# Attention's norm of half 0 ahead of half 1's mixing, and gathered rows added around the wait for the turned gates

## The reference, cut to what matters

```python
x = x + 0.5 * ffn(layernorm(x))            # L0: r = sigmoid(xr W_r), out = r * (relu(xk W_k)^2 W_v)
x = x + attention(layernorm(x))            # L0: 8 heads of 16, bias, softmax over 1,024 keys
x = x + 0.5 * ffn(layernorm(x))            # L0 again
x = x + 0.5 * experts(layernorm(x))        # L1: router, best 2 of 16 experts
x = x + gated_delta_attention(layernorm(x))  # L1
x = x + 0.5 * experts(layernorm(x))        # L1 again
```

## Time and profile before

| what | us |
|---|---|
| median of 3 runs | 602.33 |
| lowest and highest | 601.64 and 602.38 |
| the profiled execution, its own time | 601.2 |
| its span in the trace | 599.0 |
| TensorE busy | 487.4 (81% of the span) |
| VectorE busy | 468.1 (78%) |
| ScalarE busy | 312.5 (52%) |
| GpSimd busy | 158.8 (27%) |

### The profile page before, as it was taken

One profiled execution on the slowest core, in us unless ns is written; L12 is line 12 of the kernel. 1 busy time (PEld: TensorE's weight loads), 2 busy tenths in 40 slices (PEclk: granted clock), 3 DMA queues, 4 the chain that ended last, 5 costly groups with the idle time before them and its releaser, 6 DMA issues.

```text
span 599.0 us, 9248 instructions
## 1 busy us (share of the span) xinstructions
PE 487.4 (81%) x2996; PEld 259.4 (43%) x2996; DVE 468.1 (78%) x1248; ACT 312.5 (52%) x613; POOL 158.8 (27%) x198
## 2 busy tenths in 40 slices
PE   6787989999999999899788789748786887789720
PEld 3452422222222232244364679535435444679610
DVE  4978898988878988465887978697977776888852
ACT  2355456777776777688232658527143202468800
POOL 5020030010000110001274702773101055630775
PEclk8888999999999999999987979987989888999975
DMA  6006500049705003000235295511000012454542
GB/s 209 3 1 162 96 2 0 19 103 194 259 2 146 2 0 72 2 0 2 67 131 163 82 277 162 154 48 27 2 1 0 2 36 68 145 166 139 155 127 66
DMA packets 55356, 49.31 MB, mean 82 GB/s; under 512 B 4958, under 2 KB 47502, under 8 KB 54926
## 3 DMA queue, kind: packets, MB, share of 16 engines
q1 hardware_dynamic: 34686, 31.15, 18.8%
q0 software_dynamic: 4240, 9.45, 5.7%
q10 hardware_dynamic: 16384, 8.13, 4.5%
HBM read 25.85 MB, written 20.59 MB: 78 GB/s over the span
## 4 chain that ended last, share of the span: by engine, by line
PE 37%; DVE 28%; POOL 11%; issue 9%; ACT 9%; DMA 4%; ACTq 1%; SPq 0%; POOLq 0%; DVEq 0%
PE ps L814 9%; DVE arena L862 8%; PE ps L804 7%; PE ps L761 7%; POOL rows_in L1157 7%; ACT arena L1357 5%; POOL arena L1173 2%; DVE stat L257 2%; ACT arena L1366 1%; POOL small L249 1%; DMA row<-in_rows 1%; PE ps L575 1%; DVE arena L1905 1%; DMA arena<-rows_in 1%; DVE xl L285 1%
## 5 line engine op out<-in xcount | busy, mean ns | idle before, releaser
L862 DVE TENSOR_REDUCE arena<-ps 128x1 f32<-128x1024 f32 x128 | 150.8, 1219 | 25.0 <-PE ps L761 24.7
L927 ACT ACTIVATE arena<-ps 128x512 f32<-128x512 f32 x256 | 138.4, 602 | 55.1 <-PE ps L804 52.8
L804 PE MATMUL ps<-arena 99*128 99x512 bf16 x256 | 85.5, 383 | 1.1 <-ACT arena L927 1.0
L761 PE MATMUL ps<-arena 96*128 96x512 bf16 x256 | 76.5, 381 | 7.0 <-DVE arena L862 6.7
L1173 POOL DMA_INDIRECT arena<-rows_out,route x64 | 61.2, 956 | 66.4 <-DMA rows_out<-arena 47.1
L1157 POOL DMA_INDIRECT rows_in<-xl,route x64 | 62.4, 976 | 55.2 <-DVE route L1113 37.1
L814 PE MATMUL ps<-arena 128*32 128x512 f32 x512 | 68.2, 605 | 1.9 <-ACT arena L923 1.3
L804 PEld LDWEIGHTS ps<-arena 99*128 99x128 bf16 x256 | 22.2, 98 | 72.9 <-ACT arena L927 48.9
L249 POOL TENSOR_TENSOR small<-small,nhalf 128x8 f32<-128x8 f32 x11 | 18.2, 1657 | 123.4 <-DVE small L271 123.3
L1357 ACT ACTIVATE arena<-ps,route 128x128 f32<-128x128 f32 x124 | 46.4, 461 | 5.7 <-PE ps L1238 5.7
L202 PE MATMUL ps<-zerob 128*128 128x512 bf16 x148 | 43.7, 448 | 1.4 <-POOL zerob L2100 1.4
(11 more groups left out here) (276 smaller groups left out, 786.6 us busy)
## 6 DMA issues: line engine op xcount, KB each, us to landing
arena<-rows_in SPq DMA_DIRECT2D x28, 256.0 KB, 4.5
rows_out<-arena ACTq DMA_DIRECT2D x28, 256.0 KB, 2.6
rows_in<-zerob SPq DMA_DIRECT2D x2, 1920.0 KB, 11.1
arena<-att_parts SPq DMA_DIRECT2D x12, 256.0 KB, 8.9
arena<-in_consts SPq DMA_DIRECT2D x2, 1024.0 KB
arena<-zerob SPq DMA_DIRECT2D x1, 2048.0 KB, 10.5
arena<-att_parts SPq DMA_DIRECT2D x14, 128.0 KB, 8.1
att_parts<-arena SPq DMA_DIRECT2D x6, 256.0 KB
```

The lines of the kernel that those rows point to most:

```text
L761: ins = pe.matmul(ps[:, bank + keys, :], a_qs[0:96, b, h, j * P:(j + 1) * P], a_ks[0:96, b, h, keys * 512:(keys + 1) * 512], start=True, s ...
L804: pe.matmul(ps[:, score_bank(n), :], a_ks[0:99, b, h0 + h4, i * P:(i + 1) * P], a_qs[0:99, b, h0 + h4, half * 512:(half + 1) * 512], start ...
L862: nc.vector.tensor_reduce(a_nm[:, o % 2, k:k + 1], ps[:, bank:bank + 2, :].rearrange("p a b -> p (a b)"), AX.X, ALU.max, negate=True).then ...
L927: nc.scalar.activation(a_p[:, n % 16, :], ps[:, score_bank(n), :], ACT.Exp, scale=0.25).then_inc(a.ex, 1)
```

## The change

In the opening, the statistics of `n1` half 0 come straight behind half 0's add, and half 1's mixing is cut in three pieces around the rest of that norm. The second copy of `n0` half 1's turned rows goes from VectorE to ScalarE. TensorE runs fillers, half 1's first k product, four more fillers, the turning of `n1` half 0, the second k product, the projections, and only then half 1's r and v products. Half 1 of `f0` uses banks 4 and 5 for k, r and v, so ring unit 0 waits for half 1's gate products on VectorE. ScalarE takes half 1's relu and square behind the turned rows of `n1`, and each tanh just ahead of a part 2. On VectorE both of half 1's adds and the statistics of `n1` half 1 come behind half 0's values; the end of that norm comes behind ring unit 1. The turning, the products and the values of `n1` half 1 sit one or two ring units later.

Behind `m3`, quarters 0 and 1 of half 0's gathered rows are added ahead of the copy of the turned gates, quarters 2 and 3 behind it, and the b2 product last. A semaphore `b2a` counts the b2 adds, and the turning of x for the next block waits for it. The root of `n4` half 0 is issued two fetches earlier in GpSimd's queue. `m5` keeps its order.

```diff
-        def ffn_vector_mix(dve, vs, n, f, half):
+        def ffn_vector_mix(dve, vs, n, f, half, k_parts=(0, 1), r_parts=(0, 1)):
             dve.wait_ge(n.xt_a, n.turned[half] + 1)
-            for g in range(2):
+            for g in k_parts:
                 if g:
...
                                                in1=mix_in(half, g, 1), op0=ALU.mult, op1=ALU.add).then_inc(f.mixed, 1)
-            for g in range(2):
+            for g in r_parts:
                 at = slice(512 * g, 512 * (g + 1))
...
                             pe.wait_ge(a.sel, 3 * (k // 4 + 1))
+                        if u == 0:
+                            pe.wait_ge(f0.done, 2 * B)
                         if o == 0 and k == 1:
...
             turned, pick = sem("e_bases_turned"), sem("e_tile_one_hot")
+            b2a = sem("e_b2_added")
             gw, gwt, gwc, gb = sem("e_gate_rows"), sem("e_gate_rows_turned"), sem("e_gate_rows_in"), sem("e_b2_by_gates")
...
-        def moe_vector_b2(dve, vs, pair):
+        def moe_vector_gate_rows(dve, vs, pair):
...
                 nc.vector.tensor_tensor(r_oh[m.b][:, 0], r_oh[m.b][:, 0], r_oh[m.b][:, 1], ALU.add).then_inc(Moe.gw, 1)
+
+        def moe_vector_gate_rows_in(dve, pair):
             turn = pair[1].i // B + 1
...
                 ins = nc.vector.tensor_tensor(xq, xq, ps[:, b2_bank(m.b, q), :].rearrange("p (a b) -> p a b", a=4), ALU.add)
-            vs.step(ins)
+            ins.then_inc(Moe.b2a, 1)
+            dve.wait_ge(Moe.b2a, m.i + 1)
...
                 self.pe.wait_ge(self.m.added, 4 * self.m.i + 2 * g + 2)
+                self.pe.wait_ge(Moe.b2a, self.m.i + 1)
                 for j in range(4):
...
-        n0, f0 = Norm((0, 1), (0, 1), (0, 1)), Ffn(0, [places((20480, 7)), places((4096, 4), (12288, 3))], (0, 1, 0, 1), (2, 3, 2, 3), (4, 5, 4, 5))
+        n0, f0 = Norm((0, 1), (0, 1), (0, 1)), Ffn(0, [places((20480, 7)), places((4096, 4), (12288, 3))], (0, 1, 4, 5), (2, 3, 4, 5), (4, 5, 4, 5))
         n1 = Norm((2, 3), (2, 3), (2, 3), ((6, 7), (0, 1)))
...
             moe_pool_fetch(pool, m3[0])
-            moe_pool_fetch(pool, m3[1], {6: lambda: norm_pool_root(pool, n4, 0)})
+            moe_pool_fetch(pool, m3[1], {4: lambda: norm_pool_root(pool, n4, 0)})
             norm_pool_root(pool, n4, 1)
...
                 att_tensor_select(pe, 3 * (u // 8 + 1) + u % 8 // 2)
-            elif u in (4, 6):
+            elif u in (8, 10):
                 pe.wait_ge(a.r1, 1)
-                norm_tensor(pe, n1, 1, ((u - 4) // 2,))
-            elif u in (10, 12):
-                att_tensor_qk(pe, 1, 0, ((u - 10) // 2,))
-            elif u in (20, 22):
-                att_tensor_qk(pe, 1, 1, ((u - 20) // 2,))
-            elif 24 <= u < 28:
-                att_tensor_v(pe, 1, (2 * u - 48, 2 * u - 47))
+                norm_tensor(pe, n1, 1, ((u - 8) // 2,))
+            elif u in (14, 16):
+                att_tensor_qk(pe, 1, 0, ((u - 14) // 2,))
+            elif u in (22, 24):
+                att_tensor_qk(pe, 1, 1, ((u - 22) // 2,))
+            elif 26 <= u < 30:
+                att_tensor_v(pe, 1, (2 * u - 52, 2 * u - 51))
...
-        def vector_between(vs):
+        def vector_between(vs, second):
             stats = Chain(norm_vector_stats(nc.vector, vs, n2, 0, False))
...
             def between(dve, u):
-                if u == 3:
+                if u == 1:
+                    vs.finish(second)
+                if u == 5:
                     norm_vector_xt(dve, n1, 1, permuted=True, affine=True)
...
             ffn_vector_add(dve, vs, f0, 0)
-            norm_vector_xt(dve, n0, 1)
-            ffn_vector_mix(dve, vs, n0, f0, 1)
-            vs.finish(Chain(norm_vector_stats(dve, vs, n1, 0, True)))
-            ffn_vector_add(dve, vs, f0, 1, (0,))
+            norms = Chain(norm_vector_stats(dve, vs, n1, 0, True))
+            for _ in range(VARIANCE_DONE):
+                vs.advance(norms)
+            ffn_vector_mix(dve, vs, n0, f0, 1, (0,), ())
             dve.wait_ge(s_get, 1)
             nc.vector.tensor_copy(ge[:, :, :], ps[0:NE, 1, 0:2 * P].rearrange("p (a b) -> p a b", a=2)).then_inc(s_ge, 1)
+            vs.finish(norms)
+            ffn_vector_mix(dve, vs, n0, f0, 1, (1,), ())
             norm_vector_xt(dve, n1, 0, permuted=True, affine=True)
-            ffn_vector_add(dve, vs, f0, 1, (1,))
-            norms = Chain(norm_vector_stats(dve, vs, n1, 1, True))
-            for _ in range(7):
-                vs.advance(norms)
-            att_vector_rest(dve, 0, 0)
-            for _ in range(2):
-                vs.advance(norms)
-            att_vector_rest(dve, 0, 1)
-            att_vector_part3(dve, 0, 0)
-            vs.advance(norms)
-            att_vector_part3(dve, 0, 1)
+            ffn_vector_mix(dve, vs, n0, f0, 1, ())
+            for i in range(2):
+                att_vector_rest(dve, 0, i)
+            for i in range(2):
+                att_vector_part3(dve, 0, i)
             dve.wait_ge(s_wvs, 2)
             att_vector_values(dve, 0)
-            vs.finish(norms)
+            ffn_vector_add(dve, vs, f0, 1)
+            norms = Chain(norm_vector_stats(dve, vs, n1, 1, True))
+            for _ in range(VARIANCE_DONE):
+                vs.advance(norms)
             slots = Chain(moe_vector_slots(dve, vs, m3[0]))
...
                     vs.advance(slots)
-            att_vector(dve, vs, vector_between(vs), vector_in_last_octet, behind_last_values)
+            att_vector(dve, vs, vector_between(vs, norms), vector_in_last_octet, behind_last_values)
             dve.wait_ge(a.stored[3], 48)
...
             def behind_m3():
-                moe_vector_b2(dve, vs, m3)
+                moe_vector_gate_rows(dve, vs, m3)
+                moe_vector_add(dve, vs, m3[0], (0, 1))
+                moe_vector_gate_rows_in(dve, m3)
+                moe_vector_add(dve, vs, m3[0], (2, 3))
                 moe_vector_b2_add(dve, vs, m3[0])
-                moe_vector_add(dve, vs, m3[0])
                 norms = Chain(norm_vector_stats(dve, vs, n4, 0, False, False))
...
             def behind_m5():
-                moe_vector_b2(dve, vs, m5)
+                moe_vector_gate_rows(dve, vs, m5)
+                moe_vector_gate_rows_in(dve, m5)
                 for m in m5:
...
             norm_scalar_xt(act, n0, 1)
-            ffn_scalar_k(act, f0, 1)
-            ffn_scalar_r(act, f0, 1)
+            norm_scalar_xt_second(act, n0, 1)
             norm_scalar_apply(act, n1, 0)
             norm_scalar_xt(act, n1, 0, permuted=True, affine=True)
+            ffn_scalar_k(act, f0, 1)
             for i in range(2):
...
             for i in range(2):
+                ffn_scalar_r(act, f0, 1, (i,))
                 att_scalar_part2(act, 0, i)
...
             norm_tensor(pe, n0, 1)
-            ffn_tensor_k(pe, f0, 1)
-            ffn_tensor_r(pe, f0, 1)
-            ffn_tensor_v(pe, f0, 1)
-            pe.wait_ge(f0.relu, 4)
+            pe.wait_ge(f0.relu, 2)
             for i, name in enumerate(("g1", "be1")):
...
             ins.then_inc(s_get, 1)
+            keep_clock(pe, 0, 9)
+            ffn_tensor_k(pe, f0, 1, (0,))
+            keep_clock(pe, 0, 4)
             norm_tensor(pe, n1, 0)
+            ffn_tensor_k(pe, f0, 1, (1,))
             pe.wait_ge(s_ge, 1)
             att_tensor_project(pe, n1, 0)
+            ffn_tensor_r(pe, f0, 1)
+            ffn_tensor_v(pe, f0, 1)
             for i in range(3):
```

## The result

The changed kernel is slower: 605.02 us in the median of 21 runs against 601.69 of 21 runs of the kernel before. The ratio is 1.0062 with a 95% interval of 1.0043 to 1.0081, that is, +2.6 to +4.9 us. The median lies inside the range of 600.7 to 606.2 and just outside the forecast's own range of 602.7 to 605.0, and the difference of 3.3 us between the medians (3.7 by the ratio) is more than twice the forecast +1.5. The profiled execution took 604.46 us, its span is 602.3, against 601.2 and 599.0 before.

The account below looks back on a forecast made before the run. No engine bounds it everywhere: the opening runs through VectorE, TensorE and the ring, the stretch behind m3 through VectorE. Opening +2.5 us and rows -1.0 make +1.5, a median of 603.8 us, range 600.7 to 606.2.

Parts of the forecast that it names:

- Norm of half 0: Opening: statistics 4.71 us earlier, projection at 34.25 instead of 38.96, taking 3.6 us at full clock instead of 5.05.
- second rival: Opening: projection still at clock 0.50 because fillers and k products leave waits unfilled; 1.45 us more, 605.3 us; chance 0.14.
- Tanh ahead of part 2: Opening: r behind the values delays each tanh and its part 2; parts end at 45.2 instead of 49.24.
- Unit 0: Ring start: VectorE's postponed adds and statistics eat most of the lead; starts at 51.85, 1.0 us earlier than 52.87.
- The stop behind unit 1: Ring: ScalarE's four norm tiles delay select 3, TensorE idles about 6 us; unit 2 at 58.3, 2.8 us late.
- Units 2 to 17: Ring: nearly the same work on both engines, 22.6 us in place of 22.87.
- Behind m3: Behind the first expert pass: statistics start at 392.95 instead of 394.00, -1.0 us, with the last fetch as floor.
- The sum: Whole kernel: opening +2.5 us, gathered rows -1.0, total +1.5; median 603.8 us, own range 602.7 to 605.0; chance 0.46.
- The first: Ring catches up after its restart, VectorE losing none of 2.9 us idle; faster, 601.0 us; chance 0.32.
- The third: Behind the first expert pass: the second edit's gain does not arrive, x's turning and copies ending as before; 604.8 us; chance 0.08.

Follow-up runs that it names:

- filled pause: Changed kernel with 25 filler matmuls ahead of select 5, in TensorE's pause before ring unit 2; ratio 1.0056 to the kernel before.
- the opening alone: Changed kernel with the stretch behind m3 and the root's place put back as before; 603.25 us against 601.14, ratio 1.0044.
- the rows alone: Kernel before with only the second edit, the new order of gathered rows behind m3; ratio 0.9965.
- the selects: Changed kernel with ScalarE taking selects 3 to 5 ahead of its four norm tiles of half 1; ratio 1.0035 to the kernel before.
- the moved b2 add: Old opening, second edit behind m3, with the b2 add between quarters 2 and 3, in the last fetch's wait; ratio 0.9968, repeated 0.9975.

## Why the prediction was right or wrong

**Norm of half 0.** Right in its order, late by 1.2 us. The projection started 34.80 - 22.44 = 12.4 us behind the add where I had 11.2. The first term at fault is "the fillers are 13 matmuls in waits of TensorE", put at nothing; it is 0.85 of the 1.2 us (from the norm's last small instruction, L280, to the turning it is 2.81 us, 1.96 before). Behind the nine fillers TensorE idled 3.20 us until the first xk piece, and the k product and the next four fillers then ran at a granted clock of 0.50 (2.08 and 1.80 us), so the turning waited for them, not for the scaled tiles. My second rival had the half clock one step too late, in the projection; there it was 1.00 and the projection took 3.5 us, as I had said. The other 0.3 us is GpSimd's root. I had said that filling VectorE's wait for it costs nothing new, but it took 1.95 us in all seven profiles of the new opening, where VectorE works beside it, and 1.64 in all seven of the old one, where VectorE waits for it. GpSimd's timeline of the changed kernel:

```profile
27.96 1.95 POOL L249 TENSOR_TENSOR small<-small,nhalf 128x8 f32<-128x8 f32 x1 [13.41 <-DVE small L271]
```

**Tanh ahead of part 2.** Right as a mechanism, nearly right in size: the last part 3 ended 23.0 us behind the add where I had 22.1, and the difference is the late projection less 0.3. The run with r ahead of the values shows that this order cost 2.5 us at the parts and at unit 0.

**Unit 0.** "Only 1.0 us earlier than at 52.87": it started at 51.83, 0.4 us earlier counted from the add. The parts were 0.9 us later than forecast, and the work behind them 0.3 us shorter.

**The stop behind unit 1.** Right in every link: L280 at 54.09 (54.1), ScalarE's tiles at 54.29, select 3, TensorE's pause of 5.99 us (about 6), unit 2 at 58.52 (58.3). That the absolute times fit so well is in part luck, since the trace began 0.6 us earlier. From the add it is 3.7 us late, not 2.8.

**Units 2 to 17.** The term that was mis-sized most: I took 22.6 us, it measured 23.8 (23.65 in the second profile) against 22.9 before. The stop does not end at unit 2. The half clock goes on through unit 3 and the turning ahead of unit 4. The filled pause took 0.76 us out of this stretch, which leaves 23.0, and 0.82 ahead of unit 2; the other 0.4 us above my 22.6 was not traced to one wait. Together the opening cost 4.2 to 4.6 us where I had 2.5: 0.9 us of the difference arose ahead of unit 2, about 1.2 behind it. I had priced the half clock only up to unit 2.

The Trainium skill, page "TensorE: Matmul & The Clock Gate", Part 1, states that activity releases the throttle. The traces agree: the granted clock was 0.50 behind the 5.99 us pause without fillers and 1.00 with them. My 0.5 us for the half clock there was too little: the runs show 0.8 ahead of unit 2 and 1.6 at unit 17.

**Behind m3.** Right by the distances: -1.0 forecast, -0.6 in the first pair of profiles, -1.1 in the mean of the profiles, and the floor is the last fetch, as said. In the first pair that fetch started 5.10 us behind the last gate instruction (391.33 - 386.23), 4.64 before, which is about what the 0.6 lacks of the forecast. The edit alone is faster by 0.35% (0.05 to 0.65). In the changed kernel its gain is not shown in time.

**The sum.** +1.5 forecast. The steps as measured make 4.2 to 4.6 less 0.6 to 1.1, +3.1 to +4.0, and the timed difference is +2.6 to +4.9. The sign, the stop behind unit 1 and the wait for the last fetch were right; the size of the opening was too small by 1.7 to 2.1 us. The absolute 605.02 lies nearer to 605.3 and 604.8 of rivals 2 and 3 than to the forecast's 603.8, so the time alone would not have picked the forecast; the traces did.

**The rivals.** The first needed units 2 to 17 in under 21.1 us; they took 23.8. It was to catch up, and it lost a further 0.9 us instead. The second rival's half clock in the projection is not there (1.00). The third, that the second edit's gain does not arrive, is refuted for the old opening by the edit's own run. For the changed kernel it is open: the opening alone timed at +2.6 us (1.2 to 4.1), the rows alone at -2.1 (-3.9 to -0.3), both together at +3.7 (2.6 to 4.9), more than their sum of +0.5.

**What stays open.** Why the stages from the expert block on differ by up to 3.4 us between executions of the same code was not tried. Nor is it shown how much of a shift of unit 17 reaches the end, which the prediction took to be all of it. At the statistics of half 0's next expert block, some 213 us later, the changed kernel is 5.1 us late (272.99 behind the add, 267.87 before), but of the 1.6 us that the selects and the filled pause each won at unit 17 only 0.7 and 0.4 are left there, in one profile each.

## What to carry to other kernels

When a norm is pulled ahead of other work, follow the work that is pushed back to its next consumer on every engine: here the lead of 4.7 us was real, but four tiles on ScalarE stood ahead of three copies that the ring needed, and TensorE stopped for 6 us. A pause in TensorE can cost its length and then the half clock behind it, in whatever comes next. Before an effect is put down to fillers, look whether unfilled executions of the same code show it too: here the full clock in the projection came without any. A wait for a transfer that comes at its own time is a place for work that is ready: the b2 add in the wait for the last fetch took another 1.1 us off the mean distance (9.92 to 8.78, one profile), as much as the edit that made the wait.

## What the runs showed of the hardware that I had not expected

The half clock behind a pause of 3.20 us came although nine fillers had run just ahead of it (23.96 to 26.07 us): the k product behind the pause took 2.08 us, where a product like it takes 1.02. The granted clock was 1.00 from 25 to 28.5 us, 0.76 from 28.5 to 30 and 0.50 from 30 to 32. These fillers had not kept the clock for what came behind the pause.

GpSimd's root, one instruction on 128x8 elements, took 1.64 or 1.95 us, and this went with what VectorE did beside it: 1.95 in the seven profiles where VectorE mixes 512 columns (L385 and L386), 1.64 in the seven where it waits, and 1.64 again for the second root of the changed kernel (51.99 us), beside ring maxima. Why was not tried.

Two kinds of chip gave two times for the same program, 601 to 602 and 682 us. In the opening they agree to 0.7 us. The difference shows in the passes over the experts, where TensorE stops for up to 16 us. TensorE's timeline in the first run of the moved b2 add, on a chip with the longer time, then ScalarE's:

```profile
336.27 0.60 PE L1239 MATMUL ps<-cst,arena 128*128 128x128 f32 x4
352.45 1.86 PE L1229 MATMUL ps<-w,arena 128*128 x7 [15.58 <-ACT arena L1351]
```

```profile
343.75 0.22 ACT L1144 ACTIVATE route<-ps 128x64 f32<-128x64 f32 x1 [10.64 <-issue]
351.64 0.69 ACT L1351 ACTIVATE arena<-ps,cst 128x512 f32<-128x512 f32 x1 [7.67 <-remote]
```

TensorE waits for ScalarE's copy of the turned rows (L1351), and ScalarE is late with it for nothing that this trace shows: it idles 10.64 us ahead of a copy (L1144) whose input, the product of L1062, had ended at 333.7, and 7.67 us more behind it, which the trace puts down to "issue" and "remote". The rows that the late copy takes had been turned by 336.4. On the other kind of chip the same copy L1144 waited 0.76 us (the trace of the gathered rows alone). What held ScalarE was not tried. For this study it meant that only distances inside one stage could be carried from one chip to the other.
